# Layer 0 attention as a two-deep pipeline over batches, expert ranks placed ahead of the state-space step sizes, and layer 3's table of experts on 64 partitions

## The chip, the cores and the metric

The kernel runs on one core of one Trainium2 chip. The metric is device time in microseconds of one execution, the median of several. The core has five engines that each run their own instruction list in order: PE (TensorE, matmuls and transposes), DVE (VectorE), ACT (ScalarE), POOL (GpSimd, here mostly the issuer of gathers and scatters) and SP (SyncE, the issuer of plain DMAs). They meet only at semaphores, so an instruction that waits holds up all that stands behind it on its engine.

## The reference, cut to what matters

Four layers, each an attention-like part and a feed-forward part, both added to `x` (4 x 256 x 256) through a gate. Only the parts that the change touches are shown.

```python
# layer 0, attention: per batch, softmax over the context, then x rows times attention
query = ctx @ Wq.T + bq; key = ctx @ Wk.T + bk
attention = softmax(query @ key.T)               # 256 x 256 for each of 4 batches
x_m = einsum('bln,bmn->blm', norm(x), attention)
# layer 0, feed-forward: 64 experts, 8 for each token, at most 128 tokens an expert
probs = softmax(x2 @ gate_w.T); top_w, top_i = top_k(probs, 8)
pos = rank of the token within its expert (a running count); dropped if pos >= 128
y = (silu(xg @ w_gate) * (xg @ w_up)) @ w_down;  out[token] += y * weight
# layer 1, first part: a state-space model on the context (its scan runs beside layer 0's experts)
u = silu(conv(in_proj(ctx))); x_dbl = x_proj @ u
delta = softplus(dt_proj @ x_dbl[:8] + bias)     # "step sizes"
state = state * exp(delta * A) + delta * u * B;  y = state . C
# layer 3, feed-forward: 32 experts, 4 for each token, no tokens dropped
```

## The kernel before

All activations stay in on-chip memory. `x` lies as eight tiles of 128 tokens (`NT`), two to a batch (`TPB`); `bank[0..7]` are the eight accumulators of 128 x 512. Each engine's list is written out by hand, as Python functions that are called once per engine (`l0x_pe`, `l0x_act`, `l0x_dve` and so on); the order of the calls in them is the order of the work. The program runs through these stages:

1. `prep_*`, then layer 0's attention (`l0x_*`). For each batch b: PE writes the energies (`l0x_pe_energy`, L741), DVE takes their negated row maximum (L814), ACT exponentiates (L780), DVE scales by the reciprocal sum (L818, L820), PE transposes the result (L753), ACT copies it out (L798), PE multiplies it with the turned rows (L762), DVE adds to `x` and takes the statistics of the rows (`l0x_dve_add`, L832, L188). PE then turns the new rows (`rows_turn`, L244), ACT copies them (L250), and PE makes routing logits (`rows_logits`, L258). On ACT the second batch's exponential stands behind `prep_act` and `ssm_in_act`; on PE the energies of batch 2 stand behind the product of batch 0, and the logits of the first three batches stand together near the end. Beside this DVE runs the first half of layer 1's convolution (`ssm_conv_dve(dve, 0, 0, (b,))`, L415 and L418), a tap per batch.
2. Layer 0's routing (`f0_*`). DVE runs the four taps of the convolution's second half and only then takes the logits' maximum (L1191, L1193). ACT exponentiates (L1122), then does the state-space model's activations: `ssm_u_act` (L399), `ssm_dbl_act` (L444) and `ssm_dt_act` for both halves c = 0 and 1 (L447 to L456). DVE meanwhile picks the top 8 of each token and writes `f0_mask` (L1206). PE does `ssm_dt_pe` first (L430, L436), and then the ranks (L1056), 36 small matmuls on `f0_mask`. With the ranks DVE builds, for each of eight tiles, the one-hot tables `r_eq` (L1217) and `r_oc` (L1227), ACT scales them into `r_rhs` (L1134, L1136), and PE multiplies them into the table of slots (L1063); the tables are two deep. From the last one DVE makes `slots` (L1231).
3. Layer 0's experts in 32 pairs. POOL gathers each expert's rows by `slots` (L1025) and scatters the results (L1039), six pairs later. ACT copies the turned rows (L1144), applies tanh (L1150), and evicts (L1159). DVE gates (L1247, L1250) and, between pairs, makes the step sizes (`ssm_dt_dve`) and then layer 1's scan (L554, L565, L585), spread over the pairs by the list `f0_work`.
4. Layers 1 and 2 in full and layer 3's first part; the change does not touch them.
5. Layer 3's routing and experts (`e_*`). DVE finds the top 4 of 32 experts, counts tiles per expert, and forms for each of up to 64 tiles the number of its expert, `e_tab`, which PE later reads as addresses. `tile_experts` does that on a single partition in three parts, between the tables for tiles 1 and 2, 3 and 4, 5 and 6 (L2633, L2636, L2638). POOL then gathers (L2385) and scatters (L2376).

## Time and profile before

| | |
|---|---|
| median of 3 runs | 1319.86 us (1319.25 to 1321.8) |
| the profiled execution's own time | 1314.2 us |
| its span, first to last instruction | 1312.4 us |
| PE busy | 1082.1 us (82%) |
| DVE busy | 872.4 us (66%) |
| POOL busy | 709.7 us (54%) |
| ACT busy | 666.2 us (51%) |
| mean granted TensorE clock | 0.907 of full speed |

The busy shares are averages over stages with different limits. What counts for this change are the stages from 30 to 118 us and from 1060 to 1092 us of the span, in which no engine is busy all the time and each waits for another in turn.

### The profile page before, as it was taken

What the parts mean: (1) busy time and instruction counts of PE and PEld (TensorE: products, weight loads), DVE (VectorE), ACT (ScalarE), POOL (GpSimd) and SP (SyncE); (2) the same over time, 40 slices, a digit from 0 to 9 for tenths busy, and PEclk for the clock granted to TensorE, in tenths of its full rate; (3) what the DMA queues carried; (4) which work ended last, traced back from release to release, by engine and by line L of the source; (5) the groups of instructions that cost most, each with busy time, mean ns of one, the idle gap of its engine ahead of it and who ended that gap; (6) DMA issues with size and microseconds to landing.
All of it is one profiled execution on the core that took longest, in us unless ns stands there. A gap on an engine that the chain in (4) does not pass through costs nothing.

```text
span 1312.4 us, 18185 instructions
## 1 busy us (share of the span) xinstructions
PE 1082.1 (82%) x5380; PEld 841.4 (64%) x5381; DVE 872.4 (66%) x1543; ACT 666.2 (51%) x1702; POOL 709.7 (54%) x480
## 2 busy tenths in 40 slices
PE   6646668887765988999999999799999737999992
PEld 3525656766623655888888888665555536888781
DVE  4645989898869895566566665859997782332221
ACT  4275245454464214787777777467662125333330
POOL 1002878888733223444554445429996105888873
PEclk9768789999977998999999999979999757999996
DMA  6391789988550003111011110305443992555556
GB/s 184 95 212 59 180 217 322 269 248 217 102 146 1 0 1 95 56 50 53 22 49 55 51 51 1 101 1 150 148 137 75 282 220 65 82 83 83 82 78 130
DMA packets 141109, 146.06 MB, mean 111 GB/s; under 512 B 34180, under 2 KB 127356, under 8 KB 141028
## 3 DMA queue, kind: packets, MB, share of 16 engines
q1 hardware_dynamic: 115556, 110.71, 29.2%
q0 software_dynamic: 24384, 33.31, 15.2%
q10 hardware_dynamic: 1088, 1.05, 0.2%
q8 instruction: 40, 0.66, 0.2%
q14 instruction: 41, 0.34, 0.1%
HBM read 119.04 MB, written 25.99 MB: 111 GB/s over the span
## 4 chain that ended last, share of the span: by engine, by line
PE 45%; POOL 15%; DVE 15%; issue 12%; ACT 6%; DMA 6%; SPq 0%; ACTq 0%; POOLq 0%; DVEq 0%
PE bank L1608 4%; PE bank L1671 4%; PE bank L1704 4%; PE bank L1693 4%; PE bank L2472 4%; POOL f_sums L1039 3%; POOL arena L1025 2%; PE bank L1597 2%; PE bank L2138 2%; PE bank L1626 2%; PE bank L1682 2%; POOL y L2385 2%; POOL arena L585 2%; DMA f_sums<-arena,put 2%; DMA e_sums<-ctxT,put 2%
## 5 line engine op out<-in xcount | busy, mean ns | idle before, releaser
L565 DVE TENSOR_TENSOR_SCAN arena<-arena 128x1024 f32<-128x1024 f32 x64 | 155.3, 2426 | 8.3 <-DVE arena L554 3.9
L1039 POOL DMA_INDIRECT f_sums<-arena,put x64 | 126.7, 1980 | 23.6 <-issue 17.7
L585 POOL TENSOR_TENSOR arena<-arena 128x1024 f32<-128x1024 f32 x32 | 82.4, 2575 | 89.7 <-DVE arena L565 89.7
L1025 POOL DMA_INDIRECT arena<-y_rows,slots x64 | 79.6, 1244 | 81.6 <-DVEq L1232 60.7
L2376 POOL DMA_INDIRECT e_sums<-ctxT,put x63 | 100.0, 1587 | 24.0 <-issue 15.5
L2472 PE MATMUL bank<-arena,ssm_y 128*128 x504 | 109.7, 362 | 2.2 <-issue 1.3
L543 ACT ACTIVATE arena<-arena,ssm_A 128x255 f32<-128x255 f32 x256 | 107.9, 498 | 1.7 <-DVE arena L487 1.5
L2138 PE MATMUL bank<-yT,arena 128*128 128x512 f32 (+1 forms) x224 | 105.8, 618 | 2.2 <-ACT arena L2069 2.2
L595 PE MATMUL bank<-arena,ident 128*128 128x256 f32 x256 | 69.3, 418 | 40.7 <-DVE arena L585 37.2
L554 DVE TENSOR_TENSOR arena<-arena 128x1024 f32<-128x1024 f32 x64 | 94.4, 1475 | 0.0
L2385 POOL DMA_INDIRECT y<-y_rows,slots x63 | 61.8, 982 | 59.6 <-DVEq L2656 40.7
L2472 PEld LDWEIGHTS bank<-arena,ssm_y 128*128 128x128 f32 x504 | 85.7, 194 | 9.7 <-issue 6.0
L207 POOL TENSOR_TENSOR rstd<-var_eps,minus_half 128x2 f32<-128x2 f32 x32 | 26.4, 836 | 120.0 <-DVE var_eps L194 120.0
L2673 DVE TENSOR_SCALAR ctxT<-bank,slot_w 128x256 f32<-128x256 f32 x63 | 30.5, 484 | 88.3 <-DMA e_sums<-ctxT,put 75.4
L595 PEld LDWEIGHTS bank<-arena,ident 128*128 128x128 f32 x256 | 49.7, 203 | 58.2 <-DVE arena L585 39.9
L1862 DVE COPY arena<-bank 128x256 f32<-128x256 f32 x64 | 27.1, 424 | 79.5 <-PE bank L1693 79.5
L2138 PEld LDWEIGHTS bank<-yT,arena 128*128 128x128 f32 (+1 forms) x224 | 44.1, 198 | 48.1 <-issue 44.1
L1819 ACT ACTIVATE arena<-bank,x_nb,x_rq 128x256 f32<-128x256 f32 x128 | 71.1, 559 | 2.9 <-DVE x_nb L1887 0.6
L1704 PE MATMUL bank<-arena 128*128 128x256 f32 x256 | 66.3, 382 | 4.6 <-DVE arena L1862 4.6
L1932 POOL TENSOR_TENSOR x_rk<-x_kve,minus_half 128x8 f32<-128x8 f32 x16 | 27.9, 1742 | 73.5 <-DVE x_kve L1848 73.5
L1671 PE MATMUL bank<-arena 128*128 128x256 f32 x256 | 66.7, 384 | 0.0
L1693 PE MATMUL bank<-arena 128*128 128x256 f32 x256 | 66.5, 383 | 0.0
(342 smaller groups left out, 2792.2 us busy)
## 6 DMA issues: line engine op xcount, KB each, us to landing
arena<-bc_rows SPq DMA_DIRECT2D x64, 512.0 KB, 5.4
arena<-in_L_ffn_w_gate_dram SPq DMA_DIRECT2D x16, 256.0 KB, 3.7
arena<-in_L_ffn_w_up_dram SPq DMA_DIRECT2D x16, 256.0 KB, 4.5
arena<-in_L_ffn_w_down_dram SPq DMA_DIRECT2D x16, 256.0 KB, 5.5
x<-in_L_ffn_w_gate_dram SPq DMA_DIRECT2D x16, 256.0 KB, 3.8
y<-in_L_ffn_w_up_dram SPq DMA_DIRECT2D x16, 256.0 KB, 4.4
yT<-in_L_ffn_w_down_dram SPq DMA_DIRECT2D x16, 256.0 KB, 6.1
arena<-in_L_ffn_Wd_dram SPq DMA_DIRECT2D x1, 3072.0 KB, 18.1
```

Of the source, the lines that this page charges most:

```text
L543: last = nc.scalar.activation(ssm_decay[:, j % 2, n * S + 1:(n + 1) * S], ssm_delta[:, c, ds(b * S + 1, S - 1)], ACT.Exp, scale=ssm_A[:, m ...
L565: nc.vector.tensor_tensor_scan(ssm_h[:, j % 2, :], ssm_decay[:, j % 2, :], ssm_in, 0.0, ALU.mult, ALU.add).then_inc(s_ssm_h, 1)
L585: ops.tensor_tensor(ssm_hC_buf[:, j % 2, :], ssm_h[:, j % 2, :], ssm_C[:, g % 2, :], ALU.mult).then_inc(s_ssm_hC, 1)
L595: last = nc.tensor.matmul(bank[6 + c][:, 0:S], ident[:, :], ssm_hC_buf[:, j % 2, n * S:(n + 1) * S], start=(g == 0 and n == 0), stop=(g == ...
L1025: nc.gpsimd.indirect_dma_start(out=f0_xg[:, n % RING, e, :], out_offset=None, in_=y_rows, in_offset=bass.IndirectOffsetOnAxis(ap=slots[:, ...
L1039: nc.gpsimd.indirect_dma_start(out=f0_sums[m % SUMS], out_offset=bass.IndirectOffsetOnAxis(ap=put[:, m:m + 1], axis=0), in_=f0_ye[:, n % R ...
L1671: last = nc.tensor.matmul(bank[4 + b % 2][:, t * S:(t + 1) * S], x_qT[:, r, b * S + t * P:b * S + (t + 1) * P], x_kT[:, r, b * S:(b + 1) * ...
L1693: last = nc.tensor.matmul(bank[7][:, 0:S], x_ctx[:, TPB * b + j, :], x_PT[:, b % 2, j * S:(j + 1) * S], start=(j == 0), stop=(j == TPB - 1))
L1704: last = nc.tensor.matmul(bank[3][:, t * D:(t + 1) * D], x_OT[:, b % 2, t * P:(t + 1) * P], x_M[:, r, :], start=True, stop=True)
L2138: last = nc.tensor.matmul(bank[2 * (t % 2) + w][0:rows, :], g_T[:, k % 3, at:at + rows], yT[:, h, n * HALF:(n + 1) * HALF], start=(h == 0) ...
L2376: nc.gpsimd.indirect_dma_start(out=e_sums[t % 2], out_offset=bass.IndirectOffsetOnAxis(ap=put[:, t:t + 1], axis=0), in_=e_ye[:, t % 4, :], ...
L2472: last = nc.tensor.matmul(dst, e_xgT[:, r, h * P:(h + 1) * P], src[:, ds(which, 1), h, :].rearrange("p a (w n) -> p (a w) n", w=2), start= ...
```

## The change

Four things are done.

- **Attention as a pipeline.** Both first exponentials are issued ahead of `prep_act`, and both first maxima ahead of the loop on DVE. `l0x_pe_out` is split into the transposes (`l0x_pe_turn`) and the product; PE puts the energies of batch b + 2 between the two, DVE takes the maximum of batch b + 2 ahead of the sum of batch b - 1, and each batch's logits follow as soon as its rows are turned. The taps of the convolution's first half move one place back; the last of them, and all four of the second half, move into `f0_dve`: the last tap of c = 0 before the logits' maximum, the second half after it.
- **Ranks first.** `ssm_dt_pe` is split into `ssm_dbl_pe` (L430) and `ssm_dt_pe(pe, m, c)` (L436). The ranks come first on PE; the former goes in ahead of the slot products of tile 2, the latter for c = 0 ahead of those of tile 6, and for c = 1 behind the last of them. On ACT `ssm_dbl_act` stands ahead of tile 4's tables, `ssm_dt_act` for c = 0 behind the last tile's, and for c = 1 behind the tanh of pair 0.
- **PE's waits** for the step sizes (`s_sp_e`) move into the pairs, ahead of the second products of pair 0 and ahead of the first scan sums.
- **Layer 3's table.** Three groups of eight DVE operations on 128 x 128 elements become one operation each on 128 x 1024. The table is counted on 64 partitions (a comparison and a sum, 128 x 32) and turned into a row by one small matmul; `tile_experts` goes.

```diff
             for b in range(B):
+                l0x_pe_turn(pe, b)
+                if b + 2 < B:
+                    l0x_pe_energy(pe, b + 2)
+                l0x_pe_out(pe, b)
+                if b >= 1:
+                    rows_turn(b - 1)
                 if b >= 2:
-                    l0x_pe_energy(pe, b)
-                if b >= 1:
-                    l0x_pe_out(pe, b - 1)
-                if b >= 2:
-                    rows_turn(b - 2)
-            l0x_pe_out(pe, B - 1)
-            rows_turn(B - 2)
-            for b in range(B - 1):
-                rows_logits(b)
+                    rows_logits(b - 2)
+            rows_logits(B - 2)
             rows_turn(B - 1)
             rows_logits(B - 1)
...
+            top(0)
+            top(1)
+            for b in range(B):
                 dve.wait_ge(s_l0_exp, TPB * (b + 1))
...
+                if b + 2 < B:
+                    top(b + 2)
                 if b >= 1:
                     l0x_dve_add(dve, b - 1)
+                    ssm_conv_dve(dve, 0, 0, (b - 1,))
...
         def f0_pe(pe):
-            ssm_dt_pe(pe, 0)
             pe.wait_ge(s_f0_mask, 1)
...
             for i in range(NT):
+                if i == 2:
+                    ssm_dbl_pe(pe, 0)
+                if i == 6:
+                    ssm_dt_pe(pe, 0, 0)
                 pe.wait_ge(s_f0_rhs, i + 1)
...
-            pe.wait_ge(s_sp_e, 4)
+            ssm_dt_pe(pe, 0, 1)
             turn(*args(0))
...
                 gate_up(*args(n))
+                if n == 1:
+                    pe.wait_ge(s_sp_e, 2)
+                if n == START + 1:
+                    pe.wait_ge(s_sp_e, 4)
...
             ssm_u_act(act, 0)
-            ssm_dbl_act(act, 0)
-            for c in range(HC):
-                ssm_dt_act(act, 0, c)
             for i in range(NT):
+                if i == 4:
+                    ssm_dbl_act(act, 0)
                 act.wait_ge(s_f0_eq, i + 1)
...
             act.wait_ge(s_f0_clear, 16 * CLEARS)
+            ssm_dt_act(act, 0, 0)
             step(0, 0, 0)
...
                 silu(n, n % RING, n % 2)
+                if n == 0:
+                    ssm_dt_act(act, 0, 1)
...
             norm_dve(dve, 1)
-            ssm_conv_dve(dve, 0, 1, range(DC))
+            ssm_conv_dve(dve, 0, 0, (DC - 1,))
...
             nc.vector.tensor_tensor(f0_top[:, :], f0_top[:, :], rstd[:, :], ALU.mult).then_inc(s_f0_top, 1)
+            ssm_conv_dve(dve, 0, 1, range(DC))
...
+            dve_link(V.tensor_scalar(e_tabm[:, :], e_cum[:, :], token_1[:, 0:1], None, ALU.is_lt))
+            V.tensor_reduce(e_tabc[:, :], e_tabm[:, :], AX_X, ALU.add).then_inc(s_e_mask[0], 1)
...
-            for i in range(NT):
-                last = V.tensor_tensor(e_eq2[:, i, :, :], e_eq[:, i, :, :],
-                                       e_pos[:, i, :].unsqueeze(1).to_broadcast([P, K3, E3]), ALU.mult)
-            dve_link(last)
+            dve_link(V.tensor_tensor(e_eq2, e_eq, e_pos[:, :, :].unsqueeze(2).to_broadcast([P, NT, K3, E3]), ALU.mult))
...
-                if i in (2, 4, 6):
-                    tile_experts(i // 2 - 1)
```

How the lists read at the three places that matter. First PE in layer 0's attention, before, from the transposes of batch 0 on (L753 transposes, L762 the product, L741 energies, L244 the turning of rows, L258 logits):

```order
L753 MATMUL bank<-ident,arena 128x128 x4
L762 MATMUL bank<-arena,yT 128x256 x4
L741 MATMUL bank<-arena 128x256 x2
L753 MATMUL bank<-ident,arena 128x128 x4
L762 MATMUL bank<-arena,yT 128x256 x4
L244 MATMUL bank<-ident,x 128x128 x4
L741 MATMUL bank<-arena 128x256 x2
L753 MATMUL bank<-ident,arena 128x128 x4
L762 MATMUL bank<-arena,yT 128x256 x4
```

And the same place in the changed kernel (L764 is the product now):

```order
L753 MATMUL bank<-ident,arena 128x128 x4
L741 MATMUL bank<-arena 128x256 x2
L764 MATMUL bank<-arena,yT 128x256 x4
L753 MATMUL bank<-ident,arena 128x128 x4
L741 MATMUL bank<-arena 128x256 x2
L764 MATMUL bank<-arena,yT 128x256 x4
L244 MATMUL bank<-ident,x 128x128 x4
L753 MATMUL bank<-ident,arena 128x128 x4
L764 MATMUL bank<-arena,yT 128x256 x4
L244 MATMUL bank<-ident,x 128x128 x4
L258 MATMUL bank<-gwT,yT 128x64 x4
```

The energies of batches 2 and 3 now come one product earlier, and logits stand between two batches.

Second, PE around the slot products of layer 0's routing, before (L430 and L436 are `ssm_dt_pe`, L1056 the ranks, L1063 the products, L1074 the first turned rows of the experts):

```order
L430 MATMUL bank<-arena,xpT 40x512 x4
L436 MATMUL bank<-x_dbl,dtT 128x512 x4
L1056 MATMUL bank<-f_mask,tri 128x64
...
L1063 MATMUL bank<-arena 128x128 x64
L1074 MATMUL bank<-ident,arena 128x128 x8
```

And changed (L1077 the slot products, L1088 the first turned rows):

```order
L1066 MATMUL bank<-f_mask,tri 128x64
...
L1077 MATMUL bank<-arena 128x128 x16
L430 MATMUL bank<-arena,xpT 40x512 x4
L1077 MATMUL bank<-arena 128x128 x32
L437 MATMUL bank<-x_dbl,dtT 128x512 x2
L1077 MATMUL bank<-arena 128x128 x16
L437 MATMUL bank<-x_dbl,dtT 128x512 x2
L1088 MATMUL bank<-ident,arena 128x128 x8
```

The eight state-space matmuls that stood ahead of the ranks are spread over the slot products and the place behind them.

Third, ACT at the start of the experts in the changed kernel (L1151 and L1153 the last tile's tables, L448 to L457 `ssm_dt_act`, L1161 the copies of turned rows, L1167 the tanh of pair 0). Before, the last tile's tables were followed by the copies at once.

```order
L1151 ACTIVATE arena<-arena,token 128x8x64
L1153 ACTIVATE arena<-arena,f_w 128x64 x8
L448 ACTIVATE ssm_y<-arena,ssm_par 128x4x256
L454 ACTIVATE arena<-bank,ssm_par 128x512
L455 ACTIVATE arena<-bank,ssm_par 128x512
L456 ACT_TABLE_LOAD
...
L1161 COPY arena<-bank 128x512 x2
L1167 ACTIVATE arena<-bank 128x256
L448 ACTIVATE ssm_y<-arena,ssm_par 128x4x256
```

The step-size activations of c = 0 now stand between the last table and the first copy, those of c = 1 behind the first tanh.

## Rows read from the trace of the kernel before

**Rows 1.** Windows: us, busy time (instructions) of PE, PEld, DVE, ACT, POOL; clock, DMA
```profile
30.00:65.00 35.00, 21.73 (x104) 17.98 (x104) 23.72 (x55) 8.09 (x22) 3.02 (x4) 0.81 0.27 83
...
180.00:362.00 182.00, 146.79 (x833) 124.92 (x833) 165.91 (x151) 88.54 (x213) 149.97 (x87) 0.95 0.84 226
```

**Rows 2.** Groups by line, 30 to 61 us: busy, mean ns | idle before, releaser
```profile
L762 PE MATMUL bank<-arena,yT 128*128 128x256 f32 x32 | 10.8, 495 | 6.9 <-ACT arena L798 6.9
...
L832 DVE SCALAR_TENSOR_TENSOR x<-bank,tanh_g,x 128x512 f32<-128x512 f32 x4 | 3.0, 751 | 9.6 <-PE bank L762 9.6
...
L798 ACT COPY arena<-bank 128x512 f32<-128x512 f32 x4 | 2.3, 583 | 0.1
```

**Rows 3.** Timeline of DVE, layer 0's routing: start, duration, what [idle before, releaser]
```profile
63.80 0.68 DVE L1191 TENSOR_REDUCE f_top<-bank 128x8 f32<-128x512 f32 x1
...
67.95 0.20 DVE L1195 RECIPROCAL f_sum<-f_sum 128x8 f32<-128x8 f32 x1 [3.27 <-ACT arena L1122]
...
83.15 0.69 DVE L1217 TENSOR_TENSOR arena<-iota_e,f_if 128x512 f32<-128x512 f32 x1 [9.05 <-PE bank L1056]
...
86.46 0.68 DVE L1217 TENSOR_TENSOR arena<-iota_e,f_if 128x512 f32<-128x512 f32 x1
...
93.91 0.69 DVE L1217 TENSOR_TENSOR arena<-iota_e,f_if 128x512 f32<-128x512 f32 x1 [4.06 <-ACT arena L1136]
...
97.82 1.23 DVE L1227 TENSOR_TENSOR arena<-iota_c,f_pos 128x1024 f32<-128x1024 f32 x1 [1.78 <-PE bank L1063]
...
117.77 0.23 DVE L1231 TENSOR_SCALAR slots<-bank 128x64 int32<-128x64 f32 x1 [2.21 <-PE bank L1063]
```

**Rows 4.** Timeline of PE, 38 to 118 us
```profile
38.80 3.78 PE L762 MATMUL bank<-arena,yT 128*128 128x256 f32 x8 [2.94 <-ACT arena L798]
...
71.72 5.48 PE L430 MATMUL bank<-arena,xpT 128*40 128x512 f32 x8 [11.88 <-ACT arena L399]
77.87 3.70 PE L436 MATMUL bank<-x_dbl,dtT 8*128 8x512 f32 x8 [0.67 <-ACT x_dbl L444]
...
93.93 8.62 PE L1063 MATMUL bank<-arena 128*128 128x128 f32 x48 [10.98 <-ACT arena L1136]
...
115.71 2.02 PE L1063 MATMUL bank<-arena 128*128 128x128 f32 x16 [1.28 <-DVE arena L1227]
```

**Rows 5.** Timeline of ACT: step sizes, the first table, the first eviction of the experts
```profile
77.72 1.15 ACT L447 ACTIVATE ssm_y<-arena,ssm_par 128x1024 f32<-128x1024 f32 x1
...
85.28 1.13 ACT L447 ACTIVATE ssm_y<-arena,ssm_par 128x1024 f32<-128x1024 f32 x1
...
91.26 0.71 ACT L1134 ACTIVATE arena<-arena,token 128x512 f32<-128x512 f32 x1
...
133.81 0.84 ACT L1159 ACTIVATE arena<-bank,slot_w 128x256 f32<-128x256 f32 x2 [0.48 <-PE bank L1097]
```

**Rows 6.** Timeline of POOL: the first gather and the first scatter of layer 0's experts
```profile
118.36 1.20 POOL L1025 DMA_INDIRECT arena<-y_rows,slots  x1 [60.74 <-DVEq L1232]
...
136.13 1.63 POOL L1039 DMA_INDIRECT f_sums<-arena,put  x1 [0.30 <-issue]
```

**Rows 7.** Groups of POOL by line, 118 to 365 us, columns as in rows 2
```profile
L1039 POOL DMA_INDIRECT f_sums<-arena,put x62 | 123.2, 1988 | 23.0 <-issue 17.1 <-DMA f_sums<-arena,put 4.3 <-ACT arena L1159 1.7
L1025 POOL DMA_INDIRECT arena<-y_rows,slots x64 | 79.6, 1244 | 81.6 <-DVEq L1232 60.7 <-issue 18.0 <-PE bank L1074 2.6
```

**Rows 8.** Timeline of DVE, layer 3's routing
```profile
1060.66 1.71 DVE L2590 TENSOR_TENSOR yT<-iota_e,g_idxf 128x128 f32<-128x128 f32 x8
...
1075.64 2.27 DVE L2633 TENSOR_TENSOR yT<-iota_e,e_cum 1x2048 f32<-1x2048 f32 x1
...
1080.39 2.27 DVE L2636 TENSOR_REDUCE e_sig<-yT 1x64 f32<-1x2048 f32 x1
```

**Rows 9.** Timeline of PE, layer 3's slot products, cold and warm
```profile
1086.02 3.68 PE L2421 MATMUL bank<-ssm_y 128*128 128x128 f32 x16 [0.19 <-ACT ssm_y L2530]
1090.17 1.16 PE L2421 MATMUL bank<-ssm_y 128*128 128x128 f32 x8 [0.48 <-ACT ssm_y L2530]
```

More of the change, by code:

```diff
@@ L432, in ssm_dt_pe @@
                 last.then_inc(s_sp_dblp, 1)
+        def ssm_dt_pe(pe, m, c):
             pe.wait_ge(s_sp_dbl, 2 * m + 2)
-            for c in range(HC):
-                for h in range(2):
-                    nc.tensor.matmul(ssm_bank(2 * c + h)[:, :], dtT[:, HC * m + c, :],
-                                     x_dbl[0:DR, h * HALF:(h + 1) * HALF], start=True, stop=True).then_inc(s_sp_dtp, 1)
+            for h in range(2):
+                nc.tensor.matmul(ssm_bank(2 * c + h)[:, :], dtT[:, HC * m + c, :],
+                                 x_dbl[0:DR, h * HALF:(h + 1) * HALF], start=True, stop=True).then_inc(s_sp_dtp, 1)
         def ssm_dbl_act(act, m):
@@ L774, in l0x_act, with exponential @@
             norm_act(act, 0)
-            for b in range(B):
+            def exponential(b):
                 act.wait_ge(s_l0_top, b + 1)
@@ L782, in l0x_act @@
                                          accum_out=att_sum[:, b % 2, i:i + 1]).then_inc(s_l0_exp, 1)
-                if b == 0:
-                    prep_act(act, 4, len(prep_groups))
-                    ssm_in_act(act, 0)
-                if b >= 1:
-                    l0x_act_turn(act, b - 1)
-                if b >= 2:
-                    rows_turn_act(act, b - 2, 1, (6, 7))
-            l0x_act_turn(act, B - 1)
-            for b in range(B - 2, B):
-                rows_turn_act(act, b, 1, (6, 7))
+            exponential(0)
+            exponential(1)
+            prep_act(act, 4, len(prep_groups))
+            ssm_in_act(act, 0)
+            for b in range(B):
+                l0x_act_turn(act, b)
+                if b + 2 < B:
+                    exponential(b + 2)
+                if b >= 1:
+                    rows_turn_act(act, b - 1, 1, (6, 7))
+            rows_turn_act(act, B - 1, 1, (6, 7))
         def l0x_act_turn(act, b):
@@ L809, in l0x_dve, with top @@
             ssm_in_dve(dve, 0)
-            for b in range(B):
+            def top(b):
                 dve.wait_ge(s_l0_energy, b + 1)
@@ L815, in l0x_dve @@
                                         AX_X, ALU.max, negate=True).then_inc(s_l0_top, 1)
-                ssm_conv_dve(dve, 0, 0, (b,))
+            top(0)
+            top(1)
+            for b in range(B):
                 dve.wait_ge(s_l0_exp, TPB * (b + 1))
@@ L1126, in f0_act_eng @@
             ssm_u_act(act, 0)
-            ssm_dbl_act(act, 0)
-            for c in range(HC):
-                ssm_dt_act(act, 0, c)
             for i in range(NT):
+                if i == 4:
+                    ssm_dbl_act(act, 0)
                 act.wait_ge(s_f0_eq, i + 1)
@@ L2416, in e_route_pe @@
             last.then_inc(s_e_rank[0], 1)
+            wait(pe, s_e_mask, 2)
+            nc.tensor.matmul(bank[4][0:1, E3:E3 + TILES], e_tabc[0:TILES, :], ident[0:TILES, 0:TILES],
+                             start=True, stop=True).then_inc(s_e_rank[0], 1)
             for i in range(NT):
@@ L2596, in e_dve @@
             wait(dve, s_e_mask, 1)
-            for i in range(NT):
-                last = V.tensor_tensor(e_eq2[:, i, :, :], e_eq[:, i, :, :], e_p[:, i, :].unsqueeze(1).to_broadcast([P, K3, E3]),
-                                       ALU.mult)
-            dve_link(last)
+            dve_link(V.tensor_tensor(e_eq2, e_eq, e_p[:, :, :].unsqueeze(2).to_broadcast([P, NT, K3, E3]), ALU.mult))
             dve_link(V.tensor_reduce(e_wk[:, :, :], e_eq2, AX_X, ALU.add))
@@ L2766, in _ @@
             l1_prep_pe(pe)
-            ssm_dt_pe(pe, 1)
+            ssm_dbl_pe(pe, 1)
+            for c in range(HC):
+                ssm_dt_pe(pe, 1, c)
             gated_pe(pe, 0)
```

27 lines of the change are left out of this document (10 added, 17 removed).

## The prediction

> **What bounds the kernel now.** The windows come first [rows 1]. Between 30 and 65 us, layer 0's attention and logits, PE is busy for 21.7 us and DVE for 23.7 us of 35: neither is full, so the time is a chain that passes from engine to engine. From 180 to 362 us, the experts, DVE is busy for 165.9 of 182 us and POOL for 150.0, with short pauses of issue between its DMAs; that stage has a fixed length once it has begun. So the question is at which moment it begins, and that is the moment of `slots`, at 117.77 [rows 3]: POOL's first gather follows it at 118.36 [rows 6], after 60.7 us of waiting. The groups by line say what the attention's chain lost: DVE waited 9.6 us for four products, and PE 6.9 us for the copies ahead of them [rows 2]. The timeline of DVE in the routing then shows four more waits: 3.27 us for the exponentials, 9.05 us for the ranks, 4.06 us for ACT, 1.78 us for PE [rows 3]. The 9.05 us are the two state-space groups, 5.48 and 3.70 us, that stand ahead of the ranks on PE [rows 4]; the 4.06 us are the step sizes on ACT, which run from 77.72 to 91.26 [rows 5].
>
> **Attention, up to the logits' maximum (f_top).** Nothing is removed; the order is. DVE's work from 30 us to the end of f_top is about 23.4 us. The four taps of the second half, about 4.7 us of it (from 59.1 to 63.80), go behind f_top, which leaves 18.7. ACT does the second exponential ahead of `prep_act`, about 1 us, so PE's first transposes start 1.0 us later, near 31.5 instead of 30.5. A round of one batch now costs on DVE an add with statistics (1.9), a tap (1.3) and a scaling (0.85), 4.1 us. On PE it costs transposes (0.6), the copy that it waits for (0.6 [rows 2]), a product, the turning of rows and logits (0.5 and 0.9). A product takes 10.8 / 4 = 2.7 us in the mean [rows 2], 3.78 at the lower clock [rows 4] and, at twice that clock, 1.9. A round on PE is thus 4.6 to 6.5 us, more than DVE's. I walked it through with warm products: the additions to `x` end near 37.5, 41, 45 and 49, and the fourth batch's logits and the last norm meet near 54. f_top ends near 55 and, with one product at the lower clock, at 56, against 64.5 before. **Gain 8.7.** Bounds: 4.7, if only the taps move and every wait returns, and 11, if DVE never waits (31.5 + 18.7 is 50, and the first round can't be filled).
>
> **From f_top to the ranks.** The taps of the second half, 5.1 us with their links, now stand where DVE waited 3.27 us for the exponentials. So 1.8 us of them show: **loss 1.8**. The mask is ready 7 us earlier than before, near 67. The ranks follow it at once instead of behind 9.2 us of state-space matmuls. Before they took 1.5 us at the full clock; PE has now been idle since the logits, so I take 2.1. DVE waits 2.3 us instead of 9.05: **gain 6.8**. Its loop begins near 69.4 instead of 83.15.
>
> **The eight tiles.** A tile costs DVE 3.31 us (86.46 - 83.15 [rows 3]), eight cost 26.5. The loop took 34.6 us from 83.15 to `slots`; the rest was 4.06 and 1.78 of waits and a tail of 2.2. Both waits came from ACT's step sizes, which are out of the way now. What takes their place is on PE: 5.48 us cold or about 3.5 warm ahead of tile 2, and half of 3.70 ahead of tile 6 [rows 4]. Behind a product of 2.02 us warm [rows 4] in a round of 3.31, PE has 1.3 us of room a tile, and the tables are two deep. Of the first block about 1 us reaches DVE at tile 4, and the first products, at the lower clock as at 93.93 (48 of them in 8.62 us against 6.1), are absorbed by the depth. The second block is hidden up to the last product, where it adds nothing to the tail by my walk. ACT's copies of `x_dbl`, 1.2 us, delay tile 4's table by as much as PE does, at the same time. Loop 29.7 instead of 34.6: **gain 4.9**. Bounds 2 and 7. `slots` would then come at 117.8 - 18.6, near 99.
>
> **The start of the experts.** Step sizes of c = 0 take ACT 7.6 us (77.72 to 85.28, a table load in it [rows 5]) and now lie between the last table and the first copy of turned rows. That copy waits for POOL's gather and PE's transposes, which end about 6 us behind `slots` in any case; the last table ends 2.2 us ahead of `slots`. Hidden, by about half a microsecond. The cover gone, it would cost what it overlaps less. Step sizes of c = 1, 6.0 us (85.28 to 91.26), stand behind the tanh of pair 0. DVE spends 6.5 us on the first reciprocal at that point, so pair 1 is just ready. But the eviction of pair 0, which ended at 134.65, comes some 4.5 us later, and the scatter that stood on POOL 1.5 us behind it [rows 5, 6] moves by 3. The gathers queued behind that scatter move too. POOL later waited 2.6 us for PE's transposes [rows 7], so most is taken up there. **Loss 1**, bounds 0 and 3. SP's queue holds nothing that turns critical: y_rows is issued behind the norm and needs some 13 us, which ends 30 us ahead of `slots`.
>
> **Layer 3.** Three groups of eight operations take 1.71 us each [rows 8]; one operation on 1024 elements takes 1.23 (the table at 97.82 has that size [rows 3]). That is 3 x 0.48 = 1.4 less, all on the path. The comparison and the sum for the table add 0.4 on it, by similar small operations of DVE at 0.19 each; the small matmul falls in PE's idle time. `tile_experts` goes: 2.27 + 2.27 [rows 8] and 0.35. But these stood in waits for PE and ACT: a table of DVE, 1.5 us of ACT and a product form a chain that comes back to DVE every two tiles. A product of eight takes 1.16 us warm and 1.84 cold [rows 9]. Walking that chain, the last product ends 3.6 us earlier with a warm PE and 2 with a cold one. **Gain 3.0**, bounds 1.5 and 4.5. What bounds the loop next is this chain, no longer DVE.
>
> **The sum.** 8.7 - 1.8 + 6.8 + 4.9 - 1 + 3.0 = 20.6. Against the profiled execution, 1314.2 (its span 1312.4 and 1.8 around it), that gives 1293.6. The median of the runs is 1319.86, 0.4% above the profiled one; the same difference against it gives **1299**. The stages between are chains relative to their own start, so the gain should arrive in full.
>
> **A page against the change.** POOL's issues vary: a scatter takes 1988 ns in the mean [rows 7] and 1.63 us in the row at 136.13 [rows 6]. The Trainium skill, "SBUF — State Buffer", section "SBUF: two separate sides", says that certain DVE operations and GpSimd exclude each other, each for a whole instruction, and that this starves GpSimd's descriptor writing. By that rule the new alignment of DVE and POOL could lengthen or shorten the queue; no row here can settle it in advance. Its result is the last rival below. The trace agrees in so far as the same instruction differs in length.
>
> **Rivals.**
> (a) *Part of the gain is lost to a cold PE and to new waits.* Two products of the attention at 3.78 instead of 1.9 (3.8), a cold first block in the loop with its delay at tile 4 (2 to 3), the late scatter in full (2 more), layer 3 cold (1): about 9 lost, 1308. For it: the clock was 0.81 in the attention's window [rows 1] and the product at 38.80 ran at the lower one. Against it: PE's pauses shrink.
> (b) *More than forecast*: DVE hardly waits in the attention (2.3), and loop and layer 3 reach their upper bounds (2.1 and 1.5): about 6 more, 1293.
> (c) *The change does not do what it says*: the experts' start is held by something that does not move, a weight load or y_rows. Then only layer 3 and part of the rest remain, about 1312; nothing in [rows 6] supports it, since POOL was released by `slots`.
> (d) *Slower*: POOL's queue takes over the experts. Its 62 scatters and 64 gathers lasted 123.2 and 79.6 us [rows 7]; at 1.63 and 1.0 us apiece they would be 101 and 64, so 38 us are stretch. If the new alignment adds 0.7 us a pair (22 us in 32 pairs) beyond POOL's slack, the gain is gone; with the stretch grown by three quarters, 28 us, the time is 1327. It decides once a pair's round passes 8.0 us, now 182 / 25, about 7.3. The operations on both engines are the same, so I hold it unlikely.
>
> **How the numbers follow.** Forecast, 1295 to 1304: 0.68. (a), 1304 to 1311: 0.16. (b), 1290 to 1295: 0.10. (c): 0.03. (d): 0.03. The range from 1293 to 1308 leaves out the lower part of (b), the upper of (a), (c) and (d). A measurement of this kernel tells about 0.2%, 2.6 us, from no change. Faster by more than that: 0.94; within: 0.03; slower: 0.03.
>
> **What would show it.** In the changed trace f_top near 55, the mask near 67, the ranks at once behind it with DVE's wait at 2 to 3 us, no wait for ACT's tables above 1 us, `slots` near 99 and the experts as long as before (240 us from `slots` to the end of the last scan). In layer 3, from the logits' maximum to `slots`, 3 us less. The forecast is wrong if `slots` comes early but the experts' stage grows, or if the products of the attention run near 3.8 us.

## The result, and the profile after

The changed kernel takes **1301.62 us** (median of 4 runs, 1301.09 to 1302.53), the kernel before, run beside it, 1320.83 (4 runs, 1319.25 to 1322.5): a ratio of 0.9856, 95% interval 0.9841 to 0.987, 19.2 us less. The sum had said 20.6 us and 1299. A second comparison in another session (below) gave 0.9841 (0.9809 to 0.9872), 1294.09 against 1314.88, 20.8 us less. The profiled execution of after took 1301.26 us.

DVE's timeline in the routing of layer 0, the rows that answer to [rows 3] (start, duration, what, in brackets the idle time ahead and who ended it):

```profile
53.77 0.68 DVE L1211 TENSOR_REDUCE f_top<-bank 128x8 f32<-128x512 f32 x1
...
59.26 0.20 DVE L1216 RECIPROCAL f_sum<-f_sum 128x8 f32<-128x8 f32 x1
...
64.60 0.69 DVE L1227 TENSOR_TENSOR f_mask<-arena 128x512 bf16<-128x512 f32 x1
...
67.66 0.69 DVE L1238 TENSOR_TENSOR arena<-iota_e,f_if 128x512 f32<-128x512 f32 x1 [2.26 <-PE bank L1066]
...
83.32 1.23 DVE L1248 TENSOR_TENSOR arena<-iota_c,f_pos 128x1024 f32<-128x1024 f32 x1 [0.32 <-PE bank L1077]
...
96.67 0.23 DVE L1252 TENSOR_SCALAR slots<-bank 128x64 int32<-128x64 f32 x1 [2.21 <-PE bank L1077]
```

The four waits of [rows 3] are gone or small: none for the exponentials, 2.26 us instead of 9.05 for the ranks, and 0.32 in the whole loop of eight tiles instead of 4.06 and 1.78. `slots` starts 21.1 us earlier (117.77 to 96.67).

PE's timeline of after in the attention and the loop, against [rows 4] (where the second product took 3.78 us and the first state-space block 5.48):

```profile
32.67 1.97 PE L764 MATMUL bank<-arena,yT 128*128 128x256 f32 x8
...
41.55 1.99 PE L764 MATMUL bank<-arena,yT 128*128 128x256 f32 x8 [0.68 <-ACT arena L803]
...
77.61 3.63 PE L430 MATMUL bank<-arena,xpT 128*40 128x512 f32 x8
...
90.50 1.98 PE L437 MATMUL bank<-x_dbl,dtT 8*128 8x512 f32 x4
```

All four products run at the higher clock (1.97 to 1.99 us). What the start of the experts looks like in this profile, on ACT, POOL and DVE:

```profile
108.57 0.38 ACT L1167 ACTIVATE arena<-bank 128x256 f32<-128x256 f32 x1 [2.74 <-PE bank L1100]
108.85 1.14 ACT L448 ACTIVATE ssm_y<-arena,ssm_par 128x1024 f32<-128x1024 f32 x1
...
117.15 0.38 ACT L1167 ACTIVATE arena<-bank 128x256 f32<-128x256 f32 x1 [1.73 <-remote]
117.43 0.83 ACT L1176 ACTIVATE arena<-bank,slot_w 128x256 f32<-128x256 f32 x2
```

```profile
118.53 2.60 POOL L1050 DMA_INDIRECT f_sums<-arena,put  x1 [3.80 <-ACT arena L1176]
```

```profile
117.62 0.42 DVE L1268 SCALAR_TENSOR_TENSOR arena<-arena,bank 128x256 f32<-128x256 f32 x1 [1.30 <-ACT arena L1167]
```

The first scatter stands 21.9 us behind `slots`, before 18.4 [rows 3, 6], and POOL waited 3.80 us for it. From the start of `slots` to the start of the last scan it took 242.0 us, before 236.3: 5.7 us of the gain were gone in this profile, where 1 was forecast. The whole pair of profiles differs by only 12.9 us of span (1312.4 and 1299.5), where the medians differ by 19.2: 21.1 won at `slots`, 5.7 lost in the stage, 3.9 lost in code that no engine's list changes, 3.2 won in layer 3's routing and 1.9 lost behind it (0.2 are left over). So what was lost had to be told from the draw of one execution. Two waits of DVE in the middle of the experts explain most of it; this is one, with ACT's row that stands ahead of it:

```profile
251.76 0.84 ACT L1176 ACTIVATE arena<-bank,slot_w 128x256 f32<-128x256 f32 x2 [4.79 <-DMA f_sums<-arena,put]
```

```profile
254.27 2.29 DVE L566 TENSOR_TENSOR_SCAN arena<-arena 128x1024 f32<-128x1024 f32 x1 [3.92 <-issue]
```

I read the two rows together: DVE waits for a decay of ACT (the profile names no releaser for that wait, but ACT's decays start at 252.49, behind this eviction), and ACT stands in the eviction until an addition issued by POOL has landed. So the question for the experiments was: is this the late first scatter, pushed through a queue without slack, or the draw of one execution?

### The profile page after: what moved, and what is told of

Read it like the earlier page. It is cut to its first block, busy times and chain, and to the rows that moved or that the text cites. A ratio compares the mean times of both kernels' runs of the same rounds, so it can differ in the third digit from the quotient of the medians.

```text
span 1299.5 us, 18166 instructions
## 1 busy us (share of the span) xinstructions
PE 1081.3 (83%) x5382; PEld 839.8 (65%) x5383; DVE 863.2 (66%) x1521; ACT 666.3 (51%) x1702; POOL 713.6 (55%) x480
## 3 DMA queue, kind: packets, MB, share of 16 engines
q0 software_dynamic: 24384, 33.31, 15.9%
## 4 chain that ended last, share of the span: by engine, by line
PE 46%; POOL 16%; DVE 13%; issue 13%; DMA 6%; ACT 4%; another core or an unknown queue 0%; SPq 0%; ACTq 0%; POOLq 0%; DVEq 0%
PE bank L1629 4%; PE bank L1725 4%; PE bank L1692 4%; PE bank L1714 4%; PE bank L2497 3%; POOL f_sums L1050 3%; PE bank L2159 3%; DMA f_sums<-arena,put 3%; POOL arena L1036 3%; POOL y L2407 2%; PE bank L1618 2%; PE bank L1647 2%; PE bank L1703 2%; POOL arena L586 2%; DMA e_sums<-ctxT,put 2%
## 5 line engine op out<-in xcount | busy, mean ns | idle before, releaser
L1036 POOL DMA_INDIRECT arena<-y_rows,slots x64 | 84.8, 1324 | 65.4 <-DVEq L1253 46.2
L2407 POOL DMA_INDIRECT y<-y_rows,slots x63 | 61.8, 982 | 57.4 <-DVEq L2662 37.5
```

Source lines behind the costliest of these rows:

```text
L1036: nc.gpsimd.indirect_dma_start(out=f0_xg[:, n % RING, e, :], out_offset=None, in_=y_rows, in_offset=bass.IndirectOffsetOnAxis(ap=slots[:, ...
```

## Experiments

"Stage" below is the time from the start of `slots` to the start of layer 0's last scan. The table has every profiled execution; "untouched" runs from POOL's addition of the bias in layer 1 (392.83 in after) to the scaling of layer 3's logits (1043.13), all of it code that no kernel here changes; "routing 3" runs from there to layer 3's `slots`.

| kernel | slots | first scatter | stage | untouched | routing 3 |
|---|---|---|---|---|---|
| before | 117.77 | +18.4 | 236.3 | 646.4 | 36.6 |
| before, again | 115.50 | +18.4 | 238.8 | 646.9 | 36.6 |
| attention alone | 112.80 | +18.4 | 237.5 | 646.3 | 36.6 |
| layer 3 alone | 117.41 | +18.4 | 236.6 | 650.3 | 33.5 |
| merging alone | 115.89 | +18.4 | 236.9 | 646.3 | 34.4 |
| routing alone | 101.49 | +19.6 | 238.0 | 646.4 | 36.6 |
| after | 96.67 | +21.9 | 242.0 | 650.3 | 33.4 |
| after, again | 97.77 | +19.8 | 238.6 | 646.3 | 33.4 |
| step sizes between | 96.61 | +21.2 | 238.8 | 650.2 | 33.5 |
| step sizes behind | 96.85 | +18.4 | 235.1 | 646.3 | 33.5 |
| the same, again | 97.88 | +18.4 | 238.8 | 650.3 | 33.5 |
| scatters sooner | 97.97 | +15.9 | 246.7 | 646.4 | 33.5 |
| POOL late | 96.77 | +27.7 | 244.0 | 647.2 | 33.4 |
| half the scatters | 97.25 | +19.8 | 230.4 | 646.4 | 33.5 |

**The parts alone.** Each of the three parts put on the kernel before. First the order of the attention (the taps of the second half stay ahead of `f_top`):

```diff
-            for b in range(B):
-                if b >= 2:
-                    l0x_pe_energy(pe, b)
+            for b in range(B):
+                l0x_pe_turn(pe, b)
+                if b + 2 < B:
+                    l0x_pe_energy(pe, b + 2)
+                l0x_pe_out(pe, b)
...
+            ssm_conv_dve(dve, 0, 0, (DC - 1,))
             ssm_conv_dve(dve, 0, 1, range(DC))
             dve.wait_ge(s_f0_logit, 1)
```

> The kernel before with the new order of layer 0's attention and logits alone: second exponential and transposes a batch earlier, taps of the first half one batch later, the second half's taps still ahead of the logits' maximum, the old routing and the old layer 3. Theory of the sum: the prediction priced this order at 8.7 us less 4.7 for the taps, so 4 us by its terms. The trace of after showed 10 us where 8.7 were forecast, so 5.3: the logits' maximum ends near 59.4 instead of 64.69, everything up to slots moves by the same 5 us (slots near 112.5), and the time is 4 to 5.5 us less than before, ratio 0.9960 to 0.9970. Rival: the order alone brings nothing without the later ranks because the state-space matmuls and the step sizes on ScalarE hold slots at 117.8; then ratio 1.000. Rival two: experts' stage takes back what comes earlier, as it seems to in after; then slots is 5 us earlier and the end only 1 to 3.

Measured: 1312.56 us against 1316.44, ratio 0.9974 (0.9957 to 0.9991). `f_top` starts at 58.76 instead of 63.80 and `slots` at 112.80 instead of 117.77: the 5 us pass through the routing undiminished, so the rival (slots held by the step sizes) is out. The profile of before was a late one up to there: against the mean of the four profiles with the old attention and routing (`f_top` 62.8, `slots` 116.6) the gain is 4.0 and 3.8 us, the 4 us of the prediction's terms. The second rival, a stage that takes some of it back, is not excluded by the time; the stage of this profile (237.5) lies within those of before (236.3 and 238.8).

Then the routing alone (taps behind the maximum, ranks first, step sizes split), with the old attention and layer 3:

```diff
-            ssm_dt_pe(pe, 0)
             pe.wait_ge(s_f0_mask, 1)
...
+                if i == 2:
+                    ssm_dbl_pe(pe, 0)
+                if i == 6:
+                    ssm_dt_pe(pe, 0, 0)
```

> The kernel before with the new order from the logits' maximum to the experts alone (second half's taps behind the maximum, ranks ahead of the state-space matmuls, step sizes of both halves after the tables); attention and layer 3 as before. By the prediction's terms: 4.7 (taps) - 1.8 + 6.8 + 4.9 - 1 = 13.6 us up to the end of the experts; by the trace of after, where the ranks to slots gained more, 21.1 - 5.3 = 15.8 at slots (near 102.0) and 15.8 less what the late first scatter costs. If the start of the experts costs 1 us as forecast, the ratio is 0.988 to 0.9895. If it costs 5 us, as the comparison of the two traces says, the ratio is 0.9915 to 0.993. From slots to the end of the last scan: 239 to 240 us by the forecast, 243 to 245 by the trace of after.

Measured: 1300.8 us, ratio 0.9879 (0.9855 to 0.9904), just below the first bracket, which its interval covers; the interval excludes the second. `slots` at 101.49, 16.3 us earlier. The two parts at `slots` add up: 5.0 + 16.3 = 21.3, and the whole had 21.1; against the means they are 3.8 + 15.2 = 19.0, and the whole 19.4. To the end of the last scan, as the expectation counts it, the stage took 240.3 us (238.0 to its start), which is the forecast's 239 to 240 and not the 243 to 245 that the trace of after suggested.

Layer 3 alone, and of it only the three merged operations:

```diff
-            for i in range(NT):
-                last = V.tensor_tensor(e_eq2[:, i, :, :], e_eq[:, i, :, :],
-                                       e_pos[:, i, :].unsqueeze(1).to_broadcast([P, K3, E3]), ALU.mult)
-            dve_link(last)
+            dve_link(V.tensor_tensor(e_eq2, e_eq, e_pos[:, :, :].unsqueeze(2).to_broadcast([P, NT, K3, E3]), ALU.mult))
```

> The kernel before with layer 3's part alone (three groups of eight operations merged, the table of experts on 64 partitions, its small matmul and no operations for it in the loop of tiles). Forecast 3.0 us less (bounds 1.5 and 4.5), ratio 0.9977; the two traces say 3.2 from the addition of the positions to slots plus the merging ahead of it, 1.0 to 1.3, so up to 4.5 us at slots. Rival: the experts of layer 3, whose scatters wait for the additions before them, give part of it back, as they did between the two traces (1.9 us); then 1 to 2.5 us remain, ratio 0.998 to 0.9992.

> The kernel before with the merging of three groups of eight operations in layer 3 alone, not the table on 64 partitions. The prediction's terms: 3 x 0.48 = 1.4 us of the 3.0, of which one group (the positions) lies in the stretch from the additions of the positions to slots and two ahead of it. l3_only measured 3.16 us less in that stretch in each of five profiles (33.45 against 36.61). By the terms l3_merge has 36.1 there and 1.0 us less ahead of it; the rest, 2.7 us, is the table. Rival: the merging saves the whole 3.16, since the table's operations stood in waits anyway; then 33.5. Ratio 0.998 to 0.9995 against before.

Measured: ratio 0.9956 (0.9935 to 0.9976) for the whole part, 0.9967 (0.995 to 0.9984) for the merging. The medians say more than the forecast (6.4 and 4.7 us), and the second ratio is below its bracket of 0.998; but each interval still reaches, at its upper end, the size that the trace gives. The trace is far sharper than the times: routing 3 takes 33.4 to 33.5 us in all nine profiles with the whole part, 36.6 in the four without it, and 34.4 with the merging alone. So the part is worth 3.2 us, of which 2.2 are the merging and 1.0 the table. (All three groups lie in that stretch; the expectation for the merging put only one there.) Nor do the experts of layer 3 give it back, as the rival had it: from layer 3's `slots` to the end of the span it takes 220.2 to 221.2 us in thirteen profiles and 222.9 in the first of after alone. The merging exceeds 3 x 0.49 = 1.5 by 0.7: in the first row of [rows 9] two tiles' products took 3.68 us late in the loop, at the lower clock, and in the profile of the merging alone only the first two tiles' did.

**Is it the draw?** The changed kernel once more:

> The changed kernel once more, unchanged, beside its two variants on the same chip and with a second profiled execution. Question: how much of the 5.7 us that the first profile lost between slots and the end of the last scan (244.3 from slots against 238.6 before), and of the 4 us between layer 0 and layer 3, belongs to the change. If they are the draw of one execution, this profile has 235 to 240 us from slots (96.7) to the start of the last scan where the first had 242.0, and 646 us where the first had 650.3 between GpSimd's addition of the bias at 392.83 and the positions of layer 3 at 1043.13. If they belong to the change, both numbers come back within 1 us. Ratio to before 0.984 to 0.988.

> The kernel before, unchanged, for a second profiled execution. The profiled execution of before took 1314.2 us and the fastest of the runs beside it 1319.25. If the stage of the experts is a steady 236 to 237.5 us with the first scatter at slots + 18.4 (as in the profiles of att_only and l3_only, which keep that part), it is so here. If it draws as widely as the changed kernel's (235 to 242), it is outside of that. Between GpSimd's addition of the bias and the positions of layer 3: 646.3 or 650.3 us, either by chance. Ratio 1.000.

Measured: 1294.09 against 1314.88, ratio 0.9841 (0.9809 to 0.9872); the kernel before again 1314.89 against 1315.41, 0.9996 (0.9979 to 1.0013). The second profile of after has a stage of 238.6 us and 646.3 in the untouched stretch: of the 5.7 us, 3.4 were draw, and so were all 3.9 us that seemed lost in the untouched stretch. That stretch takes 646.3 to 647.2 or 650.2 to 650.3 us, in kernels of every kind. Where does it open? Between the same instructions of DVE the two profiles of the changed kernel lie 2.3 us apart at the start of the stretch, 3.9 at 484.56, 5.1 from 524 on and 6.25 at its end. So 2.9 of the 4.0 us are lost by 524, and the first 1.7 of them in one group of PE, the products on line 1409 (1388 in the kernel before); after, then after again:

```profile
479.04 5.41 PE L1409 MATMUL bank<-arena 128*128 128x256 f32 x16 [1.16 <-ACT arena L1432]
```

```profile
476.79 3.72 PE L1409 MATMUL bank<-arena 128*128 128x256 f32 x16 [1.16 <-ACT arena L1432]
```

From this group on the granted clock of the same work (40.0 and 37.2 us) is 0.81 in the first and 0.88 in the second. The group goes with the level in every profile: it takes 5.41 or 6.74 us in the four with 650 us, and 3.72 in the ten with 646 or 647. The last 1.1 us follow near 960, where the same work (52.0 and 51.1 us) has a clock of 0.93 in the first and 1.00 in the second.

The kernel before draws too: its stage took 236.3 and 238.8 us, outside the steady 236 to 237.5 that was one branch of the expectation.

**Where the step sizes stand.** ACT's step sizes of the second half behind the eviction of pair 0 ("behind"), or between the tanh of pair 1 and that eviction ("between"):

```diff
-                if n == 0:
-                    ssm_dt_act(act, 0, 1)
                 if n:
                     evict(n - 1, (n - 1) % RING, (n - 1) % 2)
+                if n == 1:
+                    ssm_dt_act(act, 0, 1)
```

> The changed kernel with one move: ScalarE does the step sizes of the second half behind the eviction of pair 0, not ahead of the tables of pair 2 and that eviction. Nothing is added or removed. Theory: GpSimd's queue runs through the experts with pauses of 0.30 us only, so its 3.80 us of waiting for that eviction cannot be caught up and come back as waits of VectorE for additions (3.9 and 4.4 us at 254 and 293 us). Then the first scatter starts 3 to 3.5 us earlier against slots (near slots + 18.4 as before), slots to the end of the last scan is 240 to 241 us instead of 244.3, and the time is 3 to 4.5 us below the changed kernel's, ratio 0.9825 to 0.9835 against before. Rival: the loss in the experts is the draw of the profiled execution (GpSimd's issues stretch differently from run to run) and the queue has slack; then the first scatter is earlier and the ratio stays within 0.001 of 0.9856.

> The same kernel as dt_behind (ScalarE's step sizes of the second half behind the eviction of pair 0), beside the changed kernel on one chip. GpSimd theory: 2 to 4 us below the changed kernel, first scatter near slots + 18.4, 235 to 237 us from slots to the start of the last scan. Rival, the 7 us between the two profiles were mostly draw: within 1.5 us of the changed kernel in the medians.

> The changed kernel with the step sizes of the second half between the tanh of pair 1 and the eviction of pair 0: the tanh of pair 1 is on time, so VectorE does not wait for pair 1, but the eviction of pair 0 and with it the first scatter are as late as in the changed kernel (slots + 21 to 22). It tells GpSimd's lateness from VectorE's own wait. GpSimd theory: the time and the stage's length are those of the changed kernel less at most 1.3 us (VectorE's wait), so 2 to 3 us above dt_behind2. Rival, VectorE's wait of 1.3 us for the tanh (with the cold TensorE behind it) is all that the placement costs: the time equals dt_behind2's.

Measured: behind, 1293.73 us and ratio 0.9828 (0.9799 to 0.9856) in its first session, and 1296.32 and 0.9841 (0.9813 to 0.9869) beside the changed kernel's 1294.09. Between: 1294.05, 0.9824 (0.9796 to 0.9853). The move did what it says: POOL's first scatter comes without a wait (behind, second time), where "between" waited.

```profile
116.26 1.63 POOL L1050 DMA_INDIRECT f_sums<-arena,put  x1 [0.30 <-issue]
```

```profile
117.80 1.67 POOL L1050 DMA_INDIRECT f_sums<-arena,put  x1 [3.11 <-ACT arena L1176]
```

But the times don't part: all four intervals overlap, and one kernel had stages of 235.1 and 238.8 us. In the session that the three shared, "behind" is even 2.2 us slower than the changed kernel in the medians, and "between" 2.3 us faster than "behind", where the theory had 2 to 4 and 2 to 3 the other way; only the first session's ratio lay in its bracket. On the size of this placement the theory of 3 to 4.5 us fell; what is left may be anything from nothing to some 3 us.

**A larger dose on POOL alone.** "Behind" with twenty small memsets ahead of the first scatter, and nothing changed on the other engines:

```diff
+                if n == LATE:
+                    for k in range(FILL):
+                        pool_link(nc.gpsimd.memset(filler[:, :], 0.0))
                 if n >= LATE:
                     scatter(n - LATE)
```

> dt_behind with some 8 us of filling work on GpSimd alone, twenty small memsets of a buffer that nothing else uses, between the last gather ahead of the first scatter and that scatter; ScalarE, VectorE and TensorE keep their order. It asks whether GpSimd's queue has slack in the experts. If the queue bounds the stage, a delay of 8 us comes back nearly in full: 243 to 246 us from slots to the start of the last scan, where dt_behind had 235.05 and 238.76, and 6 to 9 us in the time against dt_behind. If VectorE bounds it and the queue has slack (its pauses of 4 to 7 us in the whole stage for additions that are still under way), the stage stays at 235 to 240 and the time within 3 us. It weighs the step of the prediction that took the late first scatter at 1 us with bounds 0 and 3.

```profile
114.82 8.83 POOL L1063 MEMSET filler<- 128x320 f32 x20
124.50 1.63 POOL L1053 DMA_INDIRECT f_sums<-arena,put  x1 [0.84 <-POOL filler L1063]
```

Measured: 1300.43 us, ratio 0.9888 (0.9868 to 0.9909), against 0.9828 and 0.9841 without the dose. The first scatter is 9.3 us later (27.7 against 18.4), the stage 7.1 longer (244.0 against the mean of 235.1 and 238.8). So about three quarters of this delay arrive at the end; against either profile of "behind" alone it is 0.56 or 0.96 of it. VectorE's own operations beside the memsets are as long as without them (one took 0.95 us instead of 0.69), so the delay comes through the queue, which has little slack. DVE waits 4.29 us at 254.89, where after has 3.92, and 2.14 at 199.04. The other late wait (4.39 here, 4.43 in after) is no sign of a late first scatter: "attention alone" has one of 4.20 and "behind" 4.17 and 3.96, all with the scatter at +18.4.

**Less work on POOL.** The changed kernel without the scatter of every second expert, whose share is missing from the output:

```diff
-                for e in range(2):
+                for e in range(1):
                     m = 2 * n + e
```

> The changed kernel with the scatter of the second expert of each pair left out (32 of 64 scatters of layer 0, and the waits for their additions); these experts' share is missing from the output, all engines' other work stays. GpSimd's queue falls from about 236 to 165 us of work. If that queue or its additions set the stage, it shrinks: VectorE has 207 us of work there and about 11 us at the start that nothing fills, so 220 to 226 us from slots to the start of the last scan instead of 238.6 to 242.0, and 15 us less time. If the stage is VectorE's own and the waits that it shows come from TensorE and ScalarE, 233 us or more.

The groups of POOL and DVE by line in the experts (busy us, mean ns, idle before and its releasers):

```profile
L1052 POOL DMA_INDIRECT f_sums<-arena,put x32 | 66.5, 2077 | 45.1 <-ACT arena L1178 39.3 <-issue 5.8
```

```profile
L566 DVE TENSOR_TENSOR_SCAN arena<-arena 128x1024 f32<-128x1024 f32 x32 | 73.4, 2292 | 5.6 <-DVE arena L555 4.7 <-ACT arena L544 0.2
```

The same line of DVE in after again, the kernel with all scatters:

```profile
L566 DVE TENSOR_TENSOR_SCAN arena<-arena 128x1024 f32<-128x1024 f32 x32 | 73.3, 2292 | 12.3 <-issue 7.4 <-DVE arena L555 4.1
```

Measured: 1284.95 us, ratio 0.9763 (0.9742 to 0.9784); the stage 230.4 us, between the two brackets. POOL now waits 39 us for ACT and, for its gathers, 24 for PE, and the 7.4 us in which DVE stood behind evictions are gone. DVE's own 206.9 us of work, the 11 at the start and small waits make up the 230. So these scatters cost the stage 8 us against the second profile of after (238.6 - 230.4) and 11.6 against the first; the ratios, 0.9763 against 0.9856 and 0.9841, say 10 to 12. That is what POOL's queue adds on top of DVE, which remains the larger bound; the 15 us that were expected are not reached.

**Reordering the queue.** "Behind" with the scatters one pair sooner among the gathers:

```diff
-            LATE = RING + 2
+            LATE = RING + 1
```

> dt_behind with GpSimd's scatters one pair sooner among its gathers (a lag of 5 pairs instead of 6). The queue's total work is the same; the additions for which ScalarE's evictions waited (up to 6 us near 285 to 290 in the changed kernel's trace) are issued some 2.5 us earlier, the gathers that stand behind them later. If those waits are set by the order within the queue, VectorE's waits for its decays near 254 and 290 us shrink and the time falls by 2 to 5 us below dt_behind2. If the queue's total is what bounds, the waits change place (TensorE then waits for gathers) and the time stays within 1 us.

Measured: 1297.88 us, ratio 0.9856 (0.9828 to 0.9883), beside "behind" at 1296.32 and 0.9841, not to be told from it by the times; but the stage is 246.7 us in the profile, 8 more than behind's second (238.8) and 12 more than its first (235.1). The medians of the two kernels, run side by side, differ by 1.6 us only, and the profiled execution (1300.08 us) was the longest of its six, so 8 us is not what the order costs in the median: how much of it is the draw is open. The waits for additions went (1.4 us of "issue" at the scans), and TensorE waited for gathers instead, 5.24 us here, with VectorE's gating 5.86 us late behind it:

```profile
281.24 1.12 PE L1088 MATMUL bank<-ident,arena 128*128 128x128 f32 x4 [5.24 <-DMA arena<-y_rows,slots]
```

```profile
286.23 0.42 DVE L1268 SCALAR_TENSOR_TENSOR arena<-arena,bank 128x256 f32<-128x256 f32 x1 [5.86 <-ACT arena L1167]
```

The waits change place, as the second branch said, and in the profile they grow too, which neither branch said. The fall of 2 to 5 us of the first branch did not come.

No variant that does all the work beats the changed kernel by more than the measurement is uncertain.

## Why the prediction held, point by point

- **Attention, 8.7 forecast.** `f_top` starts at 53.77 instead of 63.80, 10.0 us. Part of this is the profile of before: in four profiles with the old attention and the old routing it starts at 61.8 to 63.8, mean 62.8 (the product of [rows 4] at 38.80 took 3.78 us there and 2.88 to 3.78 in the others); in the eight with the whole new order of layer 0 at 53.7 to 54.9, mean 54.2. The difference is 8.5, so the term was right. The walk behind it was right too: I had the additions to `x` end near 37.5, 41, 45 and 49, and they end at 37.3, 40.8, 44.8 and 48.8. Two errors cancel in the 8.7. I added 1 us for a product at the lower clock, and none came: the products run at 1.97 to 2.00 us in every profile with the new order, and `f_top` ends at 55.1 in the mean where I had 56. And the 64.7 from which I counted is 1.0 us later than the mean of before. One reading was off: PE's round, which I took at 4.6 to 6.5 us, is 4.4 in the last two batches (41.55 to 45.94), of which 0.68 are the wait for ACT's copy; in the first two the copy is hidden by the energies of a later batch. With PE's pauses shorter the products kept the higher clock; that the one is the cause of the other is argued, no run separates them.
- **To the ranks, -1.8 and +6.8.** From the start of `f_top` to the reciprocal 4.15 us before, 5.49 after: a loss of 1.3. From the mask to the loop 9.85 and 3.06: a gain of 6.8. The term for the ranks was right to the tenth: with the two blocks gone from ahead of them, 2.26 us of the 9.05 remain, and 2.3 was forecast.
- **The eight tiles, 4.9.** 34.6 us before, 29.0 after: 5.6. The term of 1 us for the first block at tile 4 was too large; it came to 0.32, with a block of 3.63 us and not the 5.48 of [rows 4].
- **slots.** Forecast 18.6 earlier, 21.1 in the pair of profiles, and 19.4 between the means of four profiles before (116.6) and the eight with the new order (97.2).
- **Start of the experts, -1, bounds 0 and 3.** The first half of the step sizes was hidden, as forecast. The term for the second half was too small: five profiles with the first scatter at +18.4 and the old order have a mean stage of 237.2 us, the three with the changed order (after twice, routing alone) 239.5. That is 2.3 us; with "behind" and "between" put to their sides it is 2.2, four profiles against seven. Each side scatters by some 4 us, so this is about twice the uncertainty of such a difference, and the medians of one session (above) do not show it. It lies within the bounds of 0 and 3. The prediction had named a stage that grows as a sign of being wrong; the first profile of after shows it (244.3 us to the end of the last scan where 240 was expected), the second hardly (240.9). The weak step is "most is taken up there": I took 2.6 us of waiting for PE's transposes [rows 7] for slack, and they are a draw of that one profile. In the eleven other profiles with the scatter lag of before and all scatters POOL waits 0.6 us or less for them, in before again 0.6. With the slope of the dose (7.1 / 9.3) a scatter 1.2 to 3.5 us late should cost 0.9 to 2.7, which agrees. The last rival named the queue as a bound, but by way of longer issues, which did not come; its 28 us were far off.
- **Layer 3, 3.0.** 3.2, in every profile. The split was off: merging 2.2 instead of 1.4, the table 1.0 instead of 1.6. As forecast, the chain PE, ACT, DVE bounds the loop next. DVE waits 2.20 us for PE ahead of the third tile and 0.5 to 0.7 ahead of each later one:

```profile
1066.92 0.43 DVE L2654 TENSOR_TENSOR ssm_y<-iota_e,e_hif 128x256 f32<-128x256 f32 x1 [0.67 <-PE bank L2446]
...
1068.47 0.42 DVE L2654 TENSOR_TENSOR ssm_y<-iota_e,e_hif 128x256 f32<-128x256 f32 x1 [0.52 <-PE bank L2446]
```

- **The sum.** 19.4 - 2.3 + 3.2 = 20.3, against 20.6 forecast and 19.2 and 20.8 measured. The errors of the terms nearly cancelled, and that is luck: 0.5 more than forecast at the exponentials (a loss of 1.3 instead of 1.8), 0.7 more in the loop, 0.2 less at the attention, 1.3 less in the experts.
- **POOL's issues.** Did the new alignment stretch them? Scatters took 2.00 and 1.96 us in the mean in the two profiles of after and 1.99 before [rows 7]; gathers 1.32 in both, and 1.24 and 1.34 in the two profiles of before. The stretch is there: the first 14 gathers, ahead of any scatter, take 0.97 us in the mean in every one of these profiles. The alignment did not change it beyond the draw. The Trainium skill, "SBUF — State Buffer", section "SBUF: two separate sides", names a cause for such stretch, an exclusion between certain DVE operations and GpSimd; no run here isolates it. It does not come with every DVE operation, since these gathers ran beside one as long as this (after):

```profile
109.78 6.55 DVE L471 RECIPROCAL arena<-arena 128x1024 f32<-128x1024 f32 x1
```

```profile
110.04 0.94 POOL L1036 DMA_INDIRECT arena<-y_rows,slots  x1 [0.30 <-PE bank L1088]
```

What stays open: how much of the 2.3 us the place of the step sizes costs, what sets the stage's length in one execution, and what decides which clock the group on line 1409 gets.

## What to carry to other kernels

A wait on an engine is often the work queued ahead of what one waits for: look at the queue of the releaser, and put what the critical chain wants ahead of what is wanted later. Before taking a late step as absorbed, ask whether the queue behind it has slack that can be used at that place, and whether a second profile shows the same slack; this queue, which mostly pauses only 0.3 us between issues, passed on about three quarters of a delay of 9 us, although another engine is busier. And compare more than one profile of each kernel: a difference of 4 us in code that was not touched turned out to be one of two levels that both kernels draw.

## What the runs showed of the hardware

- A stretch of untouched code takes 646.3 to 647.2 or 650.2 to 650.3 us, in one kernel as in another (after: 650.3 and 646.3). In all fourteen profiles one group of 16 products of TensorE tells which: 3.72 us in the ten short ones, 5.41 or 6.74 in the four long ones.
- The same gather of 128 rows takes GpSimd 0.97 us to issue in the mean of the first 14, and 1.24 to 1.34 in the mean of all 64 in before and after.
- Dealing two kinds of DMA from one queue in another order, one pair sooner, came with a stage of 246.7 us in one profile, beside 235.1 and 238.8, with the same number of DMAs; the mean scatter took 2.06 us instead of 1.93 and 1.96. The medians differ by 1.6 us only.
- One VectorE operation on 128 x 1024 elements took 1.22 us where eight on 128 x 128 took 1.71.
- Medians of the unchanged kernel before differ between sessions by 6 us (1320.83, 1316.44, 1314.88, 1315.41), so each kernel was compared by its ratio to the kernel before, run beside it.
